# Four interleaved chains for the null products, and masks laid down by quarters of the array

## What is computed

```python
# local attention (stage B): 16 heads of 64, windows of 64 queries, each sees its own and the previous window
allow = (kpos >= 0) & (kpos <= qpos) & (qpos - kpos <= W)
sim = jnp.einsum('bhnqd,bhnkd->bhnqk', bq, bk) * DIM_HEAD ** (-0.5)
sim = jnp.where(allow, sim, NEG)                       # NEG = -1e30
attn = softmax(sim);  out = (attn @ bv) @ w_lo.T
# routed attention (stage C): a null key and a null value for each group g and head stand beside the selected ones
k = jnp.concatenate([nk, k], axis=3);  v = jnp.concatenate([nv, v], axis=3)
...
x = x + s * silu(ffn)
```

## Time and profile before

| what | value |
| --- | --- |
| three runs | 808.08, 806.57, 808.0 us; median 808.0 |
| profiled execution, its own time | 807.63 us |
| span of the trace, first to last instruction | 805.8 us (1.8 us lie around it) |
| TensorE (PE) busy | 761.4 us, 94% of the span |
| DVE, ACT, POOL busy | 462.0, 428.6, 231.6 us |
| mean granted TensorE clock | 0.995 of full speed |

### The profile page before, as it was taken

One profiled execution on the slowest core, in us unless ns is written; L12 is line 12 of the kernel. 1 busy time (PEld: TensorE's weight loads), 2 busy tenths in 40 slices (PEclk: granted clock), 3 DMA queues, 4 the chain that ended last, 5 costly groups with the idle time before them and its releaser, 6 DMA issues.

```text
span 805.8 us, 17860 instructions
## 1 busy us (share of the span) xinstructions
PE 761.4 (94%) x6210; PEld 594.6 (74%) x6245; DVE 462.0 (57%) x1024; ACT 428.6 (53%) x1574; POOL 231.6 (29%) x373
## 2 busy tenths in 40 slices
PE   3799999999999899999999999899999999999996
PEld 3578888878876565666666667778878788797875
DVE  6422333356645887777777754665564655656454
ACT  2252444432223656766676674566574756656472
POOL 1330000000003796554455531432222323122301
PEclk9999999999999999999999999999999999999999
DMA  8600000000001323333322320000000000000001
GB/s 243 265 1 2 0 0 0 0 0 0 0 1 46 88 64 79 75 77 74 77 72 72 80 55 1 1 1 1 0 0 0 2 1 1 1 0 0 0 1 52
DMA packets 22542, 28.85 MB, mean 36 GB/s; under 512 B 6224, under 2 KB 12880, under 8 KB 21840
## 3 DMA queue, kind: packets, MB, share of 16 engines
q1 hardware_dynamic: 22480, 28.04, 12.7%
HBM read 10.19 MB, written 1.05 MB: 14 GB/s over the span
## 4 chain that ended last, share of the span: by engine, by line
PE 81%; DVE 7%; ACT 6%; issue 3%; SPq 2%; POOL 1%; DVEq 1%; DMA 0%; POOLq 0%; ACTq 0%
PE ps L706 8%; PE ps L694 8%; PE ps L963 6%; PE ps L1023 6%; PE ps L1006 6%; PE ps L755 5%; PE ps L990 5%; PE ps L681 4%; PE ps L947 4%; PE ps L675 3%; PE ps L849 3%; PE ps L861 3%; PE ps L875 3%; PE ps L825 3%; ACT stage L1251 3%
## 5 line engine op out<-in xcount | busy, mean ns | idle before, releaser
L528 POOL TENSOR_TENSOR early<-stage 128x512 f32<-128x512 f32 x64 | 81.6, 1296 | 80.1 <-DVE stage L1573 68.8
L1311 ACT ACTIVATE early<-ps,nmC 128x128 f32<-128x128 f32 (+1 forms) x224 | 78.0, 368 | 45.4 <-DVE dnC L1670 45.1
L1251 ACT ACTIVATE stage<-ps,nmB 128x128 f32<-128x128 f32 x256 | 90.3, 391 | 10.4 <-DVE nmB L1607 10.3
L706 PE MATMUL ps<-stage 128*128 128x128 f32 (+2 forms) x448 | 86.0, 320 | 1.9 <-DVE stage L1502 1.8
L694 PE MATMUL ps<-stage,early 128*128 128x128 f32 (+2 forms) x448 | 86.4, 321 | 0.0
L694 PEld LDWEIGHTS ps<-stage,early 128*128 128x128 f32 x448 | 65.2, 191 | 24.5 <-issue 15.5
L706 PEld LDWEIGHTS ps<-stage 128*128 128x128 f32 x448 | 65.3, 191 | 12.8 <-issue 2.6
L1497 DVE COPY stage<-ps 128x512 f32<-128x512 f32 x32 | 22.1, 692 | 86.6 <-PE ps L681 86.6
L1258 ACT ACTIVATE stage<-ps 128x512 f32<-128x512 f32 x64 | 34.9, 594 | 66.2 <-PE ps L861 66.2
L578 POOL TENSOR_SCALAR stage<-iota,kvcol 128x128 f32<-128x128 f32 x112 | 65.6, 601 | 6.7 <-issue 6.7
L1665 DVE TENSOR_REDUCE nmC<-ps 128x4 f32<-128x512 f32 (+1 forms) x56 | 36.5, 652 | 51.6 <-PE ps L990 51.3
(11 more groups left out here) (194 smaller groups left out, 1574.5 us busy)
## 6 DMA issues: line engine op xcount, KB each, us to landing
early<-early SPq DMA_DIRECT2D x256, 64.0 KB, 2.0
x<-in_x SPq DMA_DIRECT2D x4, 256.0 KB, 3.7
stage<-in_cq SPq DMA_DIRECT2D x1, 1024.0 KB, 5.7
stage<-in_ck SPq DMA_DIRECT2D x1, 1024.0 KB, 7.7
stage<-in_cv SPq DMA_DIRECT2D x1, 1024.0 KB, 9.7
stage<-in_co SPq DMA_DIRECT2D x1, 1024.0 KB, 12.9
early<-in_wqk SPq DMA_DIRECT2D x1, 1024.0 KB, 14.9
out<-stage SPq DMA_DIRECT2D x4, 256.0 KB, 2.3
```

The lines of the kernel that those rows point to most:

```text
L528: pool.tensor_tensor(to, a, b, (ALU.subtract, ALU.add)[f]).then_inc(rot_in, 1)
L706: t = pe.matmul(ps[:, b, q0:q1], vN[:, b % 2, m, :], simA[:, b % 2, s, at:at + q1 - q0], start=False, stop=False, skip_group_check=True)
L1251: t = act.activation(pB[:, u % 2, at, :], ps[:, 4 + h, i * P:(i + 1) * P], ACT.Exp, bias=nmB[:, u % 2, at:at + 1], accum_out=rsB[:, u % 2, ...
L1311: act.activation(pC[:, k, hg, 0:n], ps[:, 5 + k, hg * P:hg * P + n], ACT.Exp, bias=nmC[:, k, hg:hg + 1], accum_out=rsC[:, k, hg:hg + 1])
```

## The change

It has two parts. In the null products the weights are now the 16-column null tensors in all four chains, the moving operand is cq or co with 128 columns, and the four chains (NK of group 0 and 1, NV of group 0 and 1) go to partitions 0, 32, 64 and 96 of bank 7, with the chain as the inner loop. NK comes out as [16, 128] then, so ACT copies it to a new tile `NKT`, `code_columns` transposes it on TensorE into bank 5, and DVE applies the gain there. In the masks each head's 128x512 matmul becomes two matmuls of 64 rows by 64 columns of the array. Two of the four need rows of the mask that lie on the other half of the partitions; a new tile `windowx` holds the mask with its halves swapped, and DVE makes it at the start of stage A.

```diff
+        windowx = sb("windowx", [P, BLK * P], BF16)
+        NKT = sb("NKT", [H, G, D])
+        s_swapped = sem("s_swapped")
+        nulls_out = sem("nulls_out")
...
                 if job == W_NULL:
                     pe.wait_ge(s_null, 1)
-                    for g in range(G):
-                        for p in range(PAIRS):
-                            pe.matmul(ps[:, 7, g * H:(g + 1) * H], cq[:, g * PAIRS + p, :], nkb[:, g, p, :],
-                                      start=(p == 0), stop=(p == PAIRS - 1))
-                        for p in range(PAIRS):
-                            t = pe.matmul(ps[0:H, 7, P * (g + 1):P * (g + 2)], nvb[:, g, p, :],
-                                          co[:, g * PAIRS + p, :], start=(p == 0), stop=(p == PAIRS - 1))
+                    for p in range(PAIRS):
+                        for i, (null, w) in enumerate(((nkb, cq), (nkb, cq), (nvb, co), (nvb, co))):
+                            g = i % G
+                            t = pe.matmul(ps[NQ * i:NQ * i + H, 7, 0:P], null[:, g, p, :], w[:, g * PAIRS + p, :],
+                                          start=(p == 0), stop=(p == PAIRS - 1))
+                            if p == PAIRS - 1 and i < 3:
+                                t.then_inc(nulls_out, 1)
...
             def code_columns():
                 pe.wait_ge(codes, 1)
+                pe.wait_ge(w_in, W_NULL + 1)
...
+                for g in range(G):
+                    pe.transpose(ps[:, 5, W + g * H:W + (g + 1) * H], NKT[:, g, :], ident[0:H, 0:H])
                 pe.transpose(ps[:, 5, 0:Q_ROWS], qhalf[rows, :], ident[rows, rows]).then_inc(code_out, 1)
...
                 if u > 0:
                     pe.wait_ge(exp_in, 2 * u)
-                for h in range(2):
-                    pe.matmul(bank(4 + h), identb[:], windowb[:], start=True, stop=True)
+                for h, odd in ((0, 0), (1, 1), (0, 1), (1, 0)):
+                    rows = slice(DH * h, DH * (h + 1))
+                    pe.matmul(ps[W * odd:W * (odd + 1), 4 + h, :], identb[rows, rows],
+                              (windowb if odd == h else windowx)[rows, :], start=True, stop=True)
...
             pe.wait_ge(vS_zero, 1)
+            pe.wait_ge(s_swapped, 2)
...
                 if job == W_NULL:
-                    for g in range(G):
-                        act.activation(NK[:, g, :], ps[:, 7, g * H:(g + 1) * H], ACT.Copy, scale=qg[:, g:g + 1])
-                    t = act.activation(NV[:], ps[0:H, 7, P:P * (1 + G)].rearrange("p (g d) -> p g d", g=G), ACT.Copy)
+                    act.wait_ge(nulls_out, 3)
+                    for i in range(2 * G):
+                        t = act.activation((NKT, NV)[i // G][:, i % G, :], ps[NQ * i:NQ * i + H, 7, 0:P], ACT.Copy)
...
             a_v(0, 0)
+            for to in range(2):
+                dve.tensor_copy(windowx[W * to:W * (to + 1), :],
+                                windowf[W * (1 - to):W * (2 - to), :]).then_inc(s_swapped, 1)
...
             dve.tensor_copy(qrow_t[:], ps[:, 5, 0:Q_ROWS])
+            for g in range(G):
+                dve.tensor_scalar(NK[:, g, :], ps[:, 5, W + g * H:W + (g + 1) * H], qg[:, g:g + 1], None, ALU.mult)
```

## The result

The changed kernel takes 795.26 us (four runs, 794.80 to 797.56) against 807.86 before: a ratio of 0.9847, 95% interval 0.9830 to 0.9865. In a second comparison, of five runs, it was 0.9846 (0.9823 to 0.9869). The forecast was 797.7, the range 795.2 to 801.8. Its gain of 10.3 us became 12.6, and the median lies only 0.06 us inside the lower end of the range.

What follows compares the result with a forecast made beforehand. TensorE was taken to hold the chain in stage A and, from unit 7, in stage B. Terms -5.1 - 5.4 + 0.1 = -10.4 us against the 808.0 median gave 797.6; forecast 797.7, range 795.2 to 801.8.

Steps and rivals of the forecast that it cites:

- Null products: Stage A: four strips overlap, so the null records hold TensorE 2.2 us instead of 7.28, a gain of 5.1 us.
- two strips at a time: Rival for the null products: only two strips overlap, 3.7 us, gain 1.5 less, 799.2 us in all; chance 0.09.
- ACT behind them: ACT's four activations after the null products use up the cover before the y product: cost 0 to 0.3 us, taken as 0.
- Casts: DVE's two 64x512 casts at the start of stage A, at most 1.4 us for both, stay hidden: no cost.
- Code columns: Two more transposes on TensorE's chain before stage B's units: cost about 0.1 us, at most 0.2.
- Masks, each: Stage B, per unit: four mask quarters stream at once, 0.31 us instead of 0.53, a gain of 0.22 us.
- How many masks count: Stage B: units 0 to 6 gain nothing; 24 masks at 0.22 plus 0.1 for unit 28 give 5.4 us.
- DVE next: Stage B: DVE's own round of 6.92 us stays below the new 7.02; rival that DVE takes over, 800.7 us, chance 0.08.
- Clock: Stage C: one fall of TensorE's clock more or less, not predictable from the rows, 1.7 us either way.
- Slower: Rival in stage B: the four bf16 mask quarters run one after the other, adding 11.0 us, 814.0 us; chance 0.06.
- pairs: Rival in stage B: two row halves block each other, so the masks give nothing, 803.0 us; chance 0.06.
- a gap of its own: Rival in stage B: scores keep a gap behind the masks, or quarters stagger; 0.13 us gained a unit, 799.9 us; chance 0.12.

Runs made afterwards that it cites:

- nulls_only: The changed kernel's null products and code columns, with the masks left as in the kernel before: ratio 0.9946 to the kernel before (0.9928 to 0.9964).
- before_again: The kernel before with no edit, run once more for a second trace: 808.42 us.

## Why the prediction was right, and where its sizes were off

- **Null products.** Right mechanism, 0.3 short: 1.87 us and not 2.2, a gain of 5.41 and not 5.1. Four full-height strips run side by side as quarters do, 0.029 us a record. The rival of two strips at a time falls; such a kernel needs 3.19. The estimate of 2.3 us from the Trainium skill's figure for three tiles was further off. nulls_only confirms the size in time: 4.4 us (2.9 to 5.8) with the costs of the code columns and of the late copies in it.
- **ACT behind them.** The cover was used up, as put; the four activations ended 1.35 us behind the nulls, by the upper end (1.3). The cost, put at nothing out of 0 to 0.3, was 0.2.
- **Casts.** Hidden, 0.88 us both.
- **Code columns.** Under-sized: "two cost about 0.1, at most 0.2", but 0.42. The two transposes take 0.22, and the one behind them rose from 0.03 to 0.20.
- **Masks, each.** Right mechanism, 0.25 us and not 0.22. Start to start, 0.19 of it lie before the first score, for which I had put 0.22, and 0.06 among the scores, which I had not counted: their loads are drawn ahead, and they hold the chain for 0.87 instead of 1.03.
- **How many masks count.** This step failed: "In units 0 to 6 DVE, ACT and POOL hold the chain: nothing." It read one execution. In before_again TensorE holds the chain from unit 2 on, at 7.24 us but for one unit, so nearly every mask counts: from unit 0 to 31 it is 221.50 against 213.90 us, 7.6 us, where the forecast put 5.4. Of the 2.2 us between them some 1.3 are masks of units 1 to 6 and the rest is their size. The first trace held a hint: its units 3 and 4 already take 7.24 us, the length of the steady ones, though the chain, which is followed back through the slow units behind them, passes over DVE and ACT there. This term of the sum is what made 10.4 too small; with it the parts are -5.4 + 0.4 + 0.2 (late y product) - 7.6 - 0.2 (unit 0) = -12.6, and 12.6 was measured. So exact a match is partly luck, since a single trace can be off by a microsecond or two. The ratios of the parts alone multiply to 0.9897 x 0.9946 = 0.9844, the changed kernel's 0.9847.
- **DVE next.** As put: its wait fell from 0.32 to 0.06. A further tenth off the masks would bring little.
- **Clock.** As put, about 1.7 either way: it cost the trace after 1.65 us more behind the null logits. A fall doesn't always cost that: the second one of before cost nothing.
- **Range.** With the sum at 797.6 the result was 2.3 us below it; that it lies in the range, by 0.06, is owed to the room left for the clock, and is luck. By its own terms (1.7 and 0.5 about 797.7) the likeliest case also ends at 799.9 and not 799.7.
- **Slower, pairs, a gap of its own.** None came. Quarters in bf16 with 512 columns overlap as fully as the scores.

## What to carry to other kernels

Read which engine holds a stretch from two executions, not one, wherever the chain lies on VectorE and GpSimd: a start within 0.01 us decided here who waits, and with it whether the masks of the first seven units counted. Small matmuls on different strips or quarters of the array cost one stream together, if neighbours in program order use different ones and stay in one shape; halving the array's width but not its height, at the price of a second change of shape, made it slower. Before a busy engine gets more, look for where its neighbour waits: the largest extra gain, some 2.2 to 2.5 us by the traces, came from moving 3.6 us of copies to where VectorE idled anyway.

## What the runs showed of the hardware that was not expected

- Records for four strips start 0.006 to 0.007 us apart and then wait for the stream of 128 f32 columns, 0.109 us.
- TensorE started four records (two matmuls) of the next chain, on another strip, beside the last four of the chain before them in the program. A semaphore on the last matmul of one chain doesn't tell that a later chain hasn't begun.
- In all 14 traces of this study (before, after and the twelve experiments) TensorE's clock falls to its lower level within 1.0 to 3.8 us of the start of the null logits, which follow a wait of 1.6 us and have 16 moving columns, and stays there for 3.4 or 6.8 us. The longer piece costs 1.6 us more to the first scores (19.95 to 20.00 us against 18.34 to 18.36, in the 13 traces where the copies lie as before). At 20.8 to 25.7 us, in the preparation, 9 of the 14 have such a fall, and their first clearing matmul starts at 32.40 to 33.56 us; in the other five it starts at 30.36 to 31.34. A fall near the end adds to this: from the first of the last sequence's products with W2C to the end it is 19.7 us in six traces and 20.6 to 21.3 in the eight in which the clock falls earliest there. That part of the spread from run to run belongs to neither part of the change, and it is why one trace's ledger is only good to a microsecond or two.
